# When normed rows are stored and the first experts' weights are loaded, in a two-layer kernel of attention and mixtures of experts

## What is computed

```python
x = x + _L0_attn_ref(_layernorm(x), wq, wk, wv, wo)          # linear attention, no softmax, D = 64
x = x + _L0_ffn_ref(_layernorm(x), gate_w, wg, wu, wd, swg, swu, swd)
x = x + _L1_attn_ref(_layernorm(x), Wq, bq, Wk, bk, Wv, bv, Wp, bp)   # 16 heads, window of 128
x = x + _L1_ffn_ref(_layernorm(x), W1, W2, Wg, bg)           # 8 experts, the best one
```

```python
logits = xf @ gate_w.T
topw, topi = jax.lax.top_k(jax.nn.softmax(logits), 2)        # two of 8 experts for each token
hg = jnp.einsum('th,ehi->eti', xf, wg); hu = jnp.einsum('th,ehi->eti', xf, wu)
eo = jnp.einsum('eti,eih->eth', silu(hg) * hu, wd)           # INTER = 352
y = jnp.einsum('te,eth->th', wdense, eo)                     # only the two chosen experts count
shared = silu(xf @ swg) * (xf @ swu) @ swd                   # an expert that sees every token
```

## Time and profile before

| | |
|---|---|
| median of 3 runs | 1426.1 us (1425.23 to 1426.56) |
| the profiled execution's own time | 1431.44 us |
| its span, first to last instruction | 1429.7 us |
| PE busy | 1360.3 us, 95% of the span |
| DVE busy | 688.2 us, 48% |
| ACT busy | 470.6 us, 33% |
| POOL busy | 447.0 us, 31% |
| mean granted clock of TensorE | 0.986 of full speed |

### The profile page before, as it was taken

The page is one execution under the profiler, slowest core; times in us unless marked ns, Lnnn a source line. Parts: engine busy times, 40 slices in busy tenths (PEclk is TensorE's granted clock), DMA queues, the critical chain, the costliest instruction groups (busy, mean ns, idle before and its releaser), DMA issues.

```text
span 1429.7 us, 23605 instructions
## 1 busy us (share of the span) xinstructions
PE 1360.3 (95%) x7605; PEld 1010.3 (71%) x7605; DVE 688.2 (48%) x2480; ACT 470.6 (33%) x947; POOL 447.0 (31%) x533
## 2 busy tenths in 40 slices
PE   6699999999999999999999999999998999999998
PEld 4366555677777777655676767666666798999998
DVE  4455446333333333436878888878786222310000
ACT  2121211121221121123667666575656412111111
POOL 2110000153222222241554454454323333333442
PEclk9899999999999999999999999999998999999999
DMA  9800100011211212143554554544441678999996
GB/s 313 287 30 30 45 0 1 19 60 60 66 60 60 67 60 60 49 118 93 145 158 133 152 157 136 153 135 147 140 136 46 256 267 311 316 329 352 339 329 221
DMA packets 89462, 208.54 MB, mean 146 GB/s; under 512 B 11229, under 2 KB 45151, under 8 KB 79360
## 3 DMA queue, kind: packets, MB, share of 16 engines
q1 hardware_dynamic: 73664, 172.19, 36.8%
q0 software_dynamic: 12096, 32.13, 7.4%
q10 hardware_dynamic: 3584, 2.71, 0.6%
HBM read 155.74 MB, written 52.17 MB: 145 GB/s over the span
## 4 chain that ended last, share of the span: by engine, by line
PE 83%; DVE 5%; issue 4%; SPq 3%; DMA 2%; ACT 2%; POOL 1%; DVEq 0%; POOLq 0%; ACTq 0%
PE psum L795 12%; PE psum L962 10%; PE psum L972 10%; PE psum L662 8%; PE psum L774 6%; PE psum L673 6%; PE psum L821 5%; PE psum L868 5%; PE psum L843 4%; PE psum L892 3%; PE psum L922 2%; PE psum L901 2%; PE psum L753 2%; PE psum L783 2%; DVE work L1824 2%
## 5 line engine op out<-in xcount | busy, mean ns | idle before, releaser
L1824 DVE CUSTOM_DVE_ANT_0 work<-psum,mask 128x384 bf16<-128x384 f32 (+1 forms) x512 | 230.8, 485 | 73.0 <-PE psum L821 71.0
L795 PE MATMUL psum<-arena,work 128*128 x568 | 184.9, 468 | 0.4 <-issue 0.4
L821 PE MATMUL psum<-kz,qT 96*128 96x384 f32 (+1 forms) x512 | 171.6, 403 | 13.9 <-DVE small L1824 12.6
L1901 POOL DMA_INDIRECT work<-normed,token_of x71 | 67.5, 951 | 334.2 <-PE psum L753 205.7
L962 PEld LDWEIGHTS psum<-arena 128*128 128x128 f32 x1248 | 145.3, 192 | 2.2 <-issue 0.4
L962 PE MATMUL psum<-arena 128*128 128x128 f32 x1248 | 146.1, 275 | 0.0
L662 PE MATMUL psum<-arena 128*128 128x512 f32 x320 | 146.0, 594 | 0.0
L972 PE MATMUL psum<-arena 128*128 128x256 f32 x624 | 142.5, 382 | 0.8 <-issue 0.8
L1203 ACT ACTIVATE arena<-psum 128x384 f32<-128x384 f32 x256 | 112.3, 493 | 91.8 <-PE psum L843 90.7
L795 PEld LDWEIGHTS psum<-arena,work 128*128 128x128 f32 x568 | 102.1, 189 | 50.8 <-issue 1.8
L821 PEld LDWEIGHTS psum<-kz,qT 96*128 96x128 f32 x512 | 90.4, 195 | 66.9 <-DVE small L1824 40.7
(11 more groups left out here) (231 smaller groups left out, 2013.1 us busy)
## 6 DMA issues: line engine op xcount, KB each, us to landing
arena<-in_w SPq DMA_DIRECT2D x78, 1024.0 KB
strips<-hi SPq DMA_DIRECT2D x64, 256.0 KB
kz<-strips SPq DMA_DIRECT2D x64, 192.0 KB, 3.1
qT<-strips SPq DMA_DIRECT2D x32, 384.0 KB, 4.7
results<-work SPq DMA_DIRECT2D x71, 128.0 KB, 1.8
strips<-lo SPq DMA_DIRECT2D x32, 256.0 KB
normed<-work SPq DMA_DIRECT2D x14, 512.0 KB, 3.4
X<-in_x SPq DMA_DIRECT2D x8, 512.0 KB, 9.5
```

What stands on the lines that cost most here:

```text
L795: m = e.matmul(psum[:, pair[u], 0:INTER], xsT0[:, b % 2, c * P:(c + 1) * P], wu0[:, bass.ds(x, 1), c, u * INTER:(u + 1) * INTER], start=(c ...
L821: m = e.matmul(psum[:, bk, at:at + w], qT[0:ROWS_S, slot, half, i * P:(i + 1) * P], kz[slot][0:ROWS_S, hd, lo_key:hi_key], start=True, sto ...
L1824: e.tensor_tensor_reduce(masked[:, n % 2, 0:w], psum[:, bank_of["scores", u, i, hd], at:at + w], mask[:, P - off:P - off + w], 1.0, MASKED ...
L1901: e.indirect_dma_start(out=xs[:, b % 3, :], out_offset=None, in_=normed[l][0:n, :], in_offset=bass.IndirectOffsetOnAxis(ap=token_of[:, l, ...
```

## The change

The wait for the transposed loads of batches 4 to 7 is taken out of SP's program. The seven weight loads are taken from their place in front of the stores and put between them. SP first waits for batch 0's normed rows and stores them, then the same for batch 1. Behind batch 1's store it asks for one weight load, and one more behind each of the next six stores. The bytes, the number of DMAs, their shapes and their semaphores stay as they were.

```diff
             for b in range(4, B):
                 e.dma_start(X[:, b * TPB:(b + 1) * TPB, 0:E], x_in[:, b, :, :]).then_inc(x_loaded[b], 16)
                 e.dma_start(xnT_all[:, b, :, :], a["xT"][:, b, :, :]).then_inc(xT_loaded[b], 16)
-            for b in range(4, B):
-                e.wait_ge(xT_loaded[b], 16)
-            for i, n in enumerate(("wg", "wu")):
-                for c in range(EC):
-                    e.dma_start(wu0[:, :, c, i * INTER:(i + 1) * INTER],
-                                a[n][:, c * P:(c + 1) * P, :].rearrange("x p n -> p x n")).then_inc(wu0_loaded, 16)
-            for c in range(DC):
-                e.dma_start(wd0[0:IC[c], :, c, :],
-                            a["wd"][:, c * P:c * P + IC[c], :].rearrange("x p n -> p x n")).then_inc(wd0_loaded, 16)
             for b in range(B):
                 keep_normed(e, 0, b)
+                if 0 < b <= 2 * EC:
+                    i, c = divmod(b - 1, EC)
+                    e.dma_start(wu0[:, :, c, i * INTER:(i + 1) * INTER],
+                                a[("wg", "wu")[i]][:, c * P:(c + 1) * P, :].rearrange("x p n -> p x n")
+                                ).then_inc(wu0_loaded, 16)
+                if 2 * EC < b:
+                    c = b - 2 * EC - 1
+                    e.dma_start(wd0[0:IC[c], :, c, :],
+                                a["wd"][:, c * P:c * P + IC[c], :].rearrange("x p n -> p x n")).then_inc(wd0_loaded, 16)
             for b in range(B - 4, B):
                 e.wait_ge(*done["out", b, TPB - 1])
```

## The result

The changed kernel took 1419.28 us, the median of 13 runs (1416.23 to 1431.47), against 1430.32 us for 13 runs of the kernel before (1425.23 to 1438.12). The ratio is 0.9936 with a 95% interval from 0.9906 to 0.9965, that is 9.2 us of 1430.3 saved (5.0 to 13.4); between the two medians lie 11.0 us, since the ratio takes in all runs. A second set of 12 runs gave 0.9940 (0.9906 to 0.9973). The forecast was faster, and it is. But 1413.9 us, with a range up to 1417.5, was too low, and the larger part of the miss is the level that I subtracted from: 1426.1 us, where this set of the kernel before has 1430.3. The changed kernel's profiled execution took 1418.97 us with a span of 1417.2.

What follows compares the result with a forecast made beforehand. PE bounds the whole; in the mix it paused for DVE's late store. Pause 9.53 plus clock 2.72 made 12.25 us, all other terms nothing: 1426.1 - 12.2 = 1413.9 us, range 1411.5 to 1417.5.

Steps and rivals of the forecast that it cites:

- What bounds the mix, and the store's place: Mix: SP issued the first store 18 us late, behind loads; DVE waited 11.1 us at line 1273, PE 9.4 at 638.
- The level: Whole kernel: the profiled execution's saving of 12.2 us was taken off the runs' median, 1426.1 us, giving 1413.9 us.
- The 12.25 us: PE, line 662 to line 630: 18.83 us against 6.58 one period later; 9.53 us pause, 2.72 us lower clock.
- So the step should run as the later one does, and nothing else is exposed: PE's step from line 662 at 55.58: without the wait it takes 6.58 us, and no other wait appears.
- another matter: PE's 3.8 us wait at line 565: DVE was busy with earlier work there; expected to stay.
- The rival with the clock's part: Mix: slow work of 2.7 us turns up in other pauses, only 9.4 us saved, 1416.7 us; chance 0.08.
- The sum for the profiled execution: Whole profiled execution: 1431.44 - 12.25 = 1419.2 us; it lay 5.3 us above the runs' median, place unknown.
- Loads later: SP's seven weight loads: the last lands by 146 us, first experts' matmul moves to 267; cost nothing.
- loads in the stores' queue: SP's queue from store 2 on: lag behind a load 3.4 to 25.4 us, at most store 5 late by 2.0; cost nothing.
- the removed wait: SP's wait for transposed loads: it held up SP alone, until about when batch 0's norm 1 ends; nothing gained or lost.
- transfers under PE's work: Loads running up to about 135 us: PE's line 662 row takes 1.88 us with DMA busy or idle; cost nothing.
- The slower rival: Stores 1, 4 and 5 late by 3.4, 3.3 and 8.7 us, 15.4 lost against 12.2 saved, 1429.3 us; chance 0.03.

Runs made afterwards that it cites:

- two_stores_first: Against the kernel before: stores of batches 0 and 1 first, then all seven loads, then six stores, transposed-loads wait gone; 1418.71 us, ratio 0.9922.
- stores_by_act: Kernel before with loads still in front of SP's stores, but ACT's queue issuing the stores of batches 0 and 1; 1418.55 us, ratio 0.9914.
- before_both_filled: Kernel before with unread matmuls filling both PE pauses, the short one at 40 us and the long one at 58 us; 1426.47 us, ratio 0.9993.
- changed_filled: Changed kernel with four unread matmuls in PE's short pause at 40 us; 1416.03 us, ratio 0.9919 to the kernel before.
- before_filled: Kernel before with ten unread matmuls in PE's long pause in front of line 638, DVE's wait for the store kept; 1426.0 us, ratio 0.9970.
- changed_again: The changed kernel run once more, unaltered, beside the kernel before; 1419.51 us, ratio 0.9940.
- before_look_1: The kernel before, unaltered, one more execution for its profile; 1426.82 us.
- before_look_2: The kernel before, unaltered, a second further execution for its profile; 1438.23 us.

## Why the prediction was right, and where it was wrong

- **What bounds the mix, and the store's place:** right. Three kernels that get the first store out sooner in three ways (the change, two_stores_first, stores_by_act) all lose the wait.
- **The level, "I take off the same 12.2 us from the median: 1426.1":** this is the step that put the time outside the range. The median of three runs was too low a base: in the set that the change was measured in, the kernel before took 1430.32 us, 4.2 us more. Even with 12.25 us saved exactly the time would have been 1418.1, above 1417.5. Three later sets of 29, 29 and 23 runs had medians of 1428.41, 1427.65 and 1427.34, with runs from 1423 to 1439, and the range took in none of that.
- **The 12.25 us:** right as what the one execution lost behind line 662 of that step, 9.5 us of pause and 2.7 us of clock. Both parts were seen by themselves: the pause by before_both_filled against changed_filled (9.3 us in absolute time, 10.2 from the same row of PE), the clock by before_filled (2.7 us in the profile).
- **"So the step should run as the later one does, and nothing else is exposed":** this is where the mechanism failed. The step does run so, in 6.58 us. But I looked only at what comes late behind the removed wait, and not at what the wait had covered in front of it. The wait ended at a time set by DMA, so a delay on PE before it was paid out of the pause. I set PE's 3.8 us at line 565 aside as "another matter". In eight of the ten profiles of kernels that have that pause unfilled and unshortened the clock fell in it or right behind it; the one I read was one of the two where it did not. With the wait gone the fall is exposed, at 1.7 us in changed_again and 2.7 in the first changed profile, both from line 565 to line 630 against changed_filled, so that 9.5 to 10.5 us are left of 12.25 in the mix. The timed runs don't decide between these and 12.25: they give 9.2 us by the ratio with an interval from 5.0 to 13.4, and 11.0 between the medians.
- **The rival with the clock's part (1416.7 us, 0.08):** its 9.4 us saved are near what came out, but by another way. In the mix the clock's time did not turn up in later pauses; it was lost in an earlier one, which the wait had hidden.
- **The sum for the profiled execution, 1419.2 us:** it agrees with the changed kernel's profiled execution (1418.97) and its median (1419.28) by luck. Up to the first expert matmul 10.6 us were saved, 1.6 of them by the fall at 219 us that did not come again. Of the 5.3 us of which "no row says where", 3.8 were the second mixture: from its first to its last matmul of line 962 it took 299.9 us there, 296.1 in the changed profile and 296.0 in both later profiles of the kernel before. Between the two, the changed execution took 1.9 us more.
- **Loads later, loads in the stores' queue, the removed wait, transfers under PE's work:** right. Each load landed within 8.9 us, the last at about 142 us for a first use at 268.9. Store 2, the first behind a load, is among the three that landed after 2.9 to 3.6 us. A load was on its way at 62 to 64 us (365 GB/s), and PE's row of line 662 at 63.52 took 1.88 us, as those of the earlier trace rows.
- **The slower rival:** nothing of it was seen, not even with seven loads in front of store 2. Its sum was wrong too: it let store 1 be late by 3.4 us, in front of which no load stands in the changed order. Without it 12.0 us would have stood against 12.2 saved, and the kernel would not have been slower.

## What to carry to other kernels

A wait that ends at a time set by something else, here a DMA, can absorb delays in front of it on the engines that meet there. When it is removed, look back as well as forward: list the pauses and slow stretches before it, since here they were paid from then on. And take such a sum from more than one execution, and its base from more than three runs: a clock that fell in one execution and not in another was up to a quarter of the gain here, and the base from three runs was off by a third of it.

## What the hardware showed beyond that

The runs of one kernel differ with their mean granted clock. Over 81 runs of the kernel before a clock lower by 0.01 goes with 12 us more (a straight line through them gives 1436.8 us at 0.978 and 1427.1 at 0.986); 25 runs of the changed kernel give the same slope. In two executions that were profiled, before_look_1 at 1426.82 and before_look_2 at 1438.23 us, most of the difference lies in the second attention. Its score matmuls of line 821, first in the one and then in the other (min/median/max ns, first and last start us):

```profile
L821 PE MATMUL psum<-kz,qT x512: 277/365/881, 647.6 to 1095.5; 96*128 96x256 f32 x86, 96*128 96x384 f32 x85
```

```profile
L821 PE MATMUL psum<-kz,qT x512: 278/364/862, 650.1 to 1107.7; 96*128 96x256 f32 x86, 96*128 96x384 f32 x85
```

The second needs 457.6 us for what the first does in 447.9. Its clock fell at 820 to 830, 880 to 890 and 940 to 950 us, each time to 0.66 over the 10 us; the first had 0.94 and 0.89 around 820 us and no fall at the other two. Why the clock falls there in some executions is not settled here. Even with a dozen runs of each kernel the interval is some 4 us either way, so a change of 9 us is seen but not sized.
